# Denominators before the units, low halves of h on VectorE, and attention spread over the feed-forward units of a fused kernel

## The reference

```python
x = x + tanh(g_xattn[0]) * wkv(w, u, layernorm(x), ctx)          # linear recurrence over 64 steps
x = x + tanh(g_ffn[0]) * ffn(layernorm(x))                       # ternary weights, silu(gate) * up, rms_norm, projection
x = x + tanh(g_xattn[1]) * attention(layernorm(x), ctx, mask)    # 64 x 64 scores for each batch, softmax
x = x + tanh(g_ffn[1]) * linear(fp8(layernorm(x)))               # one scale over all of x
```

## Time and profile before

| what | value |
|---|---|
| three timed runs | 156.12, 156.14, 159.84 us; median 156.14 |
| the profiled execution | 155.57 us, of which the span is 153.8 us |
| PE busy | 121.0 us (79%) |
| DVE busy | 110.1 us (72%) |
| ACT busy | 93.9 us (61%) |
| POOL busy | 38.6 us (25%) |

### The profile page before, as it was taken

The page is one execution under the profiler, slowest core; times in us unless marked ns, Lnnn a source line. Parts: engine busy times, 40 slices in busy tenths (PEclk is TensorE's granted clock), DMA queues, the critical chain, the costliest instruction groups (busy, mean ns, idle before and its releaser), DMA issues. The chain is left out here.

```text
span 153.8 us, 2193 instructions
## 1 busy us (share of the span) xinstructions
PE 121.0 (79%) x733; PEld 79.1 (51%) x743; DVE 110.1 (72%) x263; ACT 93.9 (61%) x170; POOL 38.6 (25%) x80
## 2 busy tenths in 40 slices
PE   6998789729989999959689966977796897764751
PEld 6986663305335556524355645644555674532550
DVE  5879997979999999648664733405649659967940
ACT  3477695255778688895576536599548736318211
POOL 7807000077000000002505370200235612110600
PEclk9999999955999999995999999999999999999999
DMA  5999900000000000000000000000000000000224
GB/s 152 291 364 362 303 18 0 0 0 0 0 0 4 2 0 0 0 0 0 4 0 2 2 4 0 0 0 0 0 0 4 0 0 0 0 2 2 69 72 136
DMA packets 7094, 6.90 MB, mean 45 GB/s; under 512 B 1320, under 2 KB 6826, under 8 KB 7082
## 3 DMA queue, kind: packets, MB, share of 16 engines
q1 hardware_dynamic: 7072, 6.75, 13.7%
q10 hardware_dynamic: 10, 0.00, 0.0%
HBM read 5.70 MB, written 1.05 MB: 44 GB/s over the span
## 5 line engine op out<-in xcount | busy, mean ns | idle before, releaser
L1235 DVE SCALAR_TENSOR_TENSOR hbuf<-ps,pscale,sil 128x512 f32<-128x512 f32 x16 | 11.9, 746 | 20.6 <-ACT sil L573 15.5
L845 PE MATMUL ps<-wT,xhi 128*128 128x512 bf16 x60 | 23.7, 395 | 1.2 <-ACT xlo L545 0.7
L846 PE MATMUL ps<-wT,xlo 128*128 128x512 bf16 x60 | 23.5, 392 | 0.3 <-issue 0.2
L406 POOL TENSOR_SCALAR ve<-mv 128x2 f32<-128x2 f32 (+2 forms) x12 | 2.9, 239 | 68.8 <-DVE mv L1117 68.6
L904 PE MATMUL ps<-wT,wgu_raw 128*128 128x256 bf16 x128 | 16.6, 273 | 0.7 <-ACT wgu_raw L586 0.7
L573 ACT ACTIVATE sil<-ps 128x512 f32<-128x512 f32 x16 | 9.5, 596 | 10.7 <-PE ps L846 10.5
L586 ACT ACTIVATE wgu_raw<-ps 128x512 f16<-128x512 f32 x16 | 9.5, 596 | 6.9 <-PE ps L884 6.9
L1111 DVE BATCH_NORM_STATS2 stats<-xs 128x6 f32<-128x256 f32 x32 | 12.3, 415 | 1.9 <-DMA xs<-in_x_dram 1.5
L904 PEld LDWEIGHTS ps<-wT,wgu_raw 128*128 128x128 f16 x128 | 12.4, 98 | 2.2 <-ACT wgu_raw L586 1.0
L1123 DVE TENSOR_SCALAR xn<-xs,mv,rstd 128x256 f32<-128x256 f32 x26 | 10.5, 446 | 3.5 <-POOL rstd L407 2.5
L534 ACT ACTIVATE wscale<-ps 128x1024 bf16<-128x1024 f32 x6 | 6.1, 1023 | 7.9 <-PE ps L767 7.9
(11 more groups left out here) (167 smaller groups left out, 266.8 us busy)
## 6 DMA issues: line engine op xcount, KB each, us to landing
wgu_raw<-in_L_ffn_w_gate_up_dram SPq DMA_DIRECT2D x4, 512.0 KB, 9.5
ctx_sb<-in_ctx_dram SPq DMA_DIRECT2D x2, 512.0 KB, 8.7
wp_raw<-in_L_ffn_w_proj_dram SPq DMA_DIRECT2D x1, 1024.0 KB, 10.4
out_dram<-xs SPq DMA_DIRECT2D x4, 256.0 KB, 2.1
xs<-in_x_dram SPq DMA_DIRECT2D x2, 256.0 KB, 2.7
xs<-in_x_dram SPq DMA_DIRECT2D x1, 512.0 KB, 8.0
wlin_raw<-in_L_ffn_weight_dram SPq DMA_DIRECT2D x1, 256.0 KB, 9.1
bias_bc<-in_L_ffn_bias_dram SPq DMA_DIRECT2D x1, 128.0 KB, 8.7
```

The costliest lines, as they stand in the source:

```text
L845: pe.matmul(ps[:, bank, :], xhi[:, h, c, o:o + P], w, start=(c == 0), stop=False)
L846: mm = pe.matmul(ps[:, bank, :], xlo[:, h, c, o:o + P], w, start=False, stop=(c == CH - 1))
L1235: dve.scalar_tensor_tensor(out=hbuf[:, b, :], in0=ps[:, 1 + b, :], scalar=pscale[:, 0:1], in1=sil[:, b, :], op0=ALU.mult, op1=ALU.mult).th ...
```

## The change

- **Denominators first.** The denominator scan and bonus of pieces 2 and 3 (`den_scan`, `den_bonus`) run on DVE before the units, and ACT runs `invert(2)` and `invert(3)` before the first silu. `rest_in(2)` moves behind `silu(0)`. Both table loads of iteration 5 go. The numerators (`num_scan`, `num_bonus`) and `wkv_out` run in iterations 3 and 4, `quant` of matrix 5 in iteration 5, `y_back(1)` in iteration 5 instead of 6, `mix_pair(2)` in 5.
- **Low halves on DVE.** For units 8 to 15 `h_left` on PE and `h_low` on ACT are gone; DVE subtracts the high half from the bank itself.
- **Tanh gates.** For units 11 to 15 ACT computes tanh(gate / 2), and `gate_product` on DVE makes (tanh + 1) * gate of it; `pscale_half` carries the factor 1/2. One table set (`exp_and_others`), loaded once in iteration 11, serves these gates and all softmax exponentials. The two loads of iteration 12 and the one after the units go.
- **Attention spread.** The two attention groups that ran in iterations 10 to 14 by pairs are spread singly over iterations 9 to 15; `ffn_in(2)` and `ffn_in(3)` stand before `h_back`, the second one in iteration 9 instead of 8. `softmax_out(1)`, `attn_out(1)` and `part_stats(3, 1)` move behind the units.
- **POOL and DVE.** The masks and the clearing of `E` move from POOL to DVE in iteration 8; POOL's `bias_g` and `mean_square(2)` stand before its four weight parts, which now wait for the squares of unit 11.

```diff
-    EXP_UNIT = 12
+    LOW_DVE = 8
+    TANH_FROM = 11
...
+        th_ready = sem("th_ready")
+        halved = sem("halved")
         h_ready = sem("h_ready")
         hhi_ready = sem("hhi_ready")
         sq_ready = sem("sq_ready")
...
+            mean_square(2)
+            pool.wait_ge(in_bias, 16)
+            pool.tensor_scalar(bias_g[:, :], bias_bc[:, :], tg[:, 3:4], 0.0, ALU.mult, ALU.add).then_inc(bias_ready, 1)
...
+            power_and_shift(3, 0, 2, 1)
             power(2, 4, 2, 3)
             mean_square(3)
+            power(2, 6, 1, 4)
             mean_square(4)
-            power_and_shift(3, 0, 2, 1)
-            power(2, 6, 1, 4)
+            power(2, 7, 1, 5)
             power_and_shift(3, 2, 2, 2)
-            power(2, 7, 1, 5)
...
             rest_in(1)
+            invert(2)
             ln_apply(1, 0, TPC // 2, 1)
             xn_high(0)
             xn_high(1)
             xn_low(0)
             xn_low(1)
-            rest_in(2)
+            invert(3)
             act.preload_act_table_set("silu_and_others")
...
-                act.activation(sil[:, n % 2, :], ps[:, 0, :], ACT.Silu).then_inc(sil_ready, 1)
+                if n < TANH_FROM:
+                    act.activation(sil[:, n % 2, :], ps[:, 0, :], ACT.Silu).then_inc(sil_ready, 1)
+                else:
+                    act.activation(sil[:, n % 2, :], ps[:, 0, :], ACT.Tanh, scale=0.5).then_inc(th_ready, 1)
...
             for n in range(UNITS):
-                if n in (6, EXP_UNIT + 1):
-                    h_high(n - 1)
+                if n == TANH_FROM:
+                    act.preload_act_table_set("exp_and_others")
                 silu(n)
                 if n >= 1:
                     square(n - 1)
-                    if n not in (6, EXP_UNIT + 1):
-                        h_high(n - 1)
-                    h_low(n - 1)
+                    if n == 7:
+                        xn_high(2)
+                    if n == 9:
+                        xn_high(3)
+                    h_high(n - 1)
+                    if n - 1 < LOW_DVE:
+                        h_low(n - 1)
                 if n == 0:
+                    rest_in(2)
                     rest_in(3)
                 if n == 1:
                     rest_in(4)
@@ -627,42 +638,31 @@
                     rest_in(5)
                 if n == 4:
                     linear_weight()
-                if n == 5:
-                    act.preload_act_table_set("natural_log_exp_and_others")
-                    invert(2)
-                    invert(3)
-                    act.preload_act_table_set("silu_and_others")
                 if n == 7:
-                    xn_high(2)
                     xn_low(2)
-                if n == 8:
-                    xn_high(3)
+                if n == 9:
                     xn_low(3)
-                if n == 10:
                     channels_in(qT, 0, qT_ps, qT_ready)
                 if n == 11:
+                    softmax_exp(0)
                     channels_in(qT, 1, qT_ps, qT_ready)
-                if n == EXP_UNIT:
-                    act.preload_act_table_set("natural_log_exp_and_others")
-                    softmax_exp(0)
+                if n == 12:
+                    attn_in(0)
+                if n == 13:
                     softmax_exp(1)
-                    act.preload_act_table_set("silu_and_others")
-                if n == EXP_UNIT + 2:
-                    attn_in(0)
+                if n == 14:
                     attn_in(1)
             square(UNITS - 1)
             h_high(UNITS - 1)
-            h_low(UNITS - 1)
-            act.preload_act_table_set("natural_log_exp_and_others")
             channels_in(qT, 2, qT_ps, qT_ready)
             ln_apply(3, 0, 2, 2)
...
@@ -1015,13 +1015,32 @@
                 if n < UNITS:
                     gate(n)
                     up(n)
+                if n == 7:
+                    ffn_in(2)
+                if n == 9:
+                    ffn_in(3)
+                if n == 10:
+                    scores(0)
+                if n == 11:
+                    channel_major(2, 1, qT_ps)
+                if n == 12:
+                    probs_back(0)
+                    scores(1)
+                if n == 13:
+                    attend(0)
+                if n == 14:
+                    probs_back(1)
+                if n == 15:
+                    attend(1)
+                if n == UNITS + 1:
+                    channel_major(2, 2, qT_ps)
                 if 1 <= n <= UNITS:
                     h_back(n - 1)
                 if n >= 2:
                     project(n - 2)
-                if n == 6:
+                if n == 5:
                     y_back(1)
-                if 1 <= n <= UNITS:
+                if 1 <= n <= LOW_DVE:
                     h_left(n - 1)
...
                 if n == 7:
-                    ffn_in(2)
                     ffn_in_left(2)
-                if n == 8:
-                    ffn_in(3)
+                if n == 9:
                     ffn_in_left(3)
-                if n == 9:
                     channel_major(2, 0, qT_ps)
-                if n == 10:
-                    channel_major(2, 1, qT_ps)
-                    scores(0)
-                if n == 11:
-                    scores(1)
-                if n == EXP_UNIT + 1:
-                    probs_back(0)
-                    probs_back(1)
-                if n == EXP_UNIT + 2:
-                    attend(0)
-                    attend(1)
-
-            channel_major(2, 2, qT_ps)
+
             scores(2)
             channel_major(2, 3, qT_ps)
             residual_back(0)
+            probs_back(2)
             scores(3)
-            probs_back(2)
+            channel_major(2, 4, qT_ps)
+            attend(2)
             residual_back(1)
...
+            def den_scan(k):
+
+                dve.wait_ge(G_ready, k + 1)
+                dve.tensor_tensor_scan(sums[:, k, 0, :, :].rearrange("p b t -> p (b t)"), dec[:, k % CH, :],
+                                       kv[:, k, 0, :, :].rearrange("p b t -> p (b t)"), 0.0, ALU.mult,
+                                       ALU.add).then_inc(den_scanned, 1)
...
+            def num_scan(k):
+
+                dve.wait_ge(GV_ready, k + 1)
+                dve.tensor_tensor_scan(sums[:, k, 1, :, :].rearrange("p b t -> p (b t)"), dec[:, k % CH, :],
+                                       kv[:, k, 1, :, :].rearrange("p b t -> p (b t)"), 0.0, ALU.mult,
+                                       ALU.add).then_inc(scan_ready, 1)
...
+            def gate_product(n):
+
+                b = n % 2
+                dve.wait_ge(th_ready, n - TANH_FROM + 1)
+                dve.scalar_tensor_tensor(out=sil[:, b, :], in0=sil[:, b, :], scalar=1.0, in1=ps[:, 0, :],
+                                         op0=ALU.add, op1=ALU.mult).then_inc(sil_ready, 1)
+
+            def h_low(n):
+                dve.wait_ge(hhi_ready, n + 1)
+                dve.tensor_tensor(hlo[:, n % 2, :], ps[:, 3, :], hhi[:, n % 2, :], ALU.subtract).then_inc(hlo_ready, 1)
...
                 b = n % 2
+                if n >= TANH_FROM:
+                    gate_product(n)
+                if n == TANH_FROM:
+                    dve.wait_ge(halved, 1)
...
-                dve.scalar_tensor_tensor(out=hbuf[:, b, :], in0=ps[:, 1 + b, :], scalar=pscale[:, 0:1],
+                dve.scalar_tensor_tensor(out=hbuf[:, b, :], in0=ps[:, 1 + b, :], scalar=(pscale if n < TANH_FROM else pscale_half)[:, 0:1],
...
+            def masks():
+                dve.wait_ge(in_mask, 32)
+                dve.tensor_scalar(mask_f[:, :, :], mask_u8[:, :, :], 1.0, 0.0, ALU.mult, ALU.add).then_inc(mask_f_ready, 1)
+                dve.memset(E[:, :, :], 0.0).then_inc(E_0, 1)
+                dve.wait_ge(mask_f_ready, 1)
+                dve.tensor_scalar(mask_add[:, :, :], mask_f[:, :, :], -1.0, MASKED, ALU.add, ALU.mult).then_inc(mask_ready, 1)
...
+            den_scan(2)
             weights_scale()
-            wkv_product(2)
             mix_out()
             ln_stats(1, 0, TPC)
+            den_bonus(2)
             greatest_scales()
             ln_apply(1, TPC // 2, TPC // 2, 1)
+            den_scan(3)
+            den_bonus(3)
...
-            wkv_scan(2)
...
-                    wkv_bonus(2)
                 if n == 3:
+                    wkv_product(2)
                     wkv_product(3)
-                    wkv_scan(3)
+                    num_scan(2)
+                    num_bonus(2)
+                    wkv_out(2)
                 if n == 4:
-                    wkv_bonus(3)
+                    num_scan(3)
+                    num_bonus(3)
+                    wkv_out(3)
+                if n == 5:
                     quant_here(5)
                     quant_sign(5)
-                if n == 5:
-                    wkv_out(2)
-                    wkv_out(3)
-                if n == 6:
                     mix_pair(2)
                     ln_stats(1, 4, 2)
+                if n == 6:
```

(27 more changed lines are left out.)

34 lines of the change are left out of this document (22 added, 12 removed).

## The result

The changed kernel takes **144.31 us**, the median of four runs (143.94 to 146.07), against 156.95 for the kernel before beside it (156.12 to 159.84, four runs). The ratio is 0.923, with a 95% interval of 0.912 to 0.935. The forecast was 144.4. The kernel before took 154.2 to 162.6 us in the runs beside the experiments, longer at a lower mean granted clock (0.967: 154.8; 0.935: about 159.5; one at 0.73: 175.2, and one of b1_den_only at 0.74: 170.9), so a time is set only beside times taken with it.

A forecast was written before the change was run, and what follows sets the result against it. No engine bounds the whole; PE waits where its order meets ACT's, and DVE has room. Terms -0.8 - 2.2 - 5.4 - 3.8 + 0.5 = -11.7 from 155.57, plus 0.5 for the median: 144.4 us, range 142.0 to 148.5.

The forecast's parts named there:

- Stretch A, the front, +1.9: Up to gate(7): rest_in(2) behind the first silu makes PE wait, so gate(1) starts at 44.3 instead of 42.37, +1.9.
- The first rival: PE's clock falls in a new gap, before weight_rest(3), the first h_left or gate(8): 146.0, two falls 147.6; chance 0.20.
- The stall of iterations 5 and 6, -2.7: Before gate(7): both loads gone and y_back moved, PE runs without the old stall, gate(7) at 66.1 instead of 68.80.
- Stretch B, the clock of unit 7, -1.6: Gate(7) to gate(8): full clock for unit 7's gate and up, -1.6; the whole stretch 5.2 us instead of 7.4, -2.2.
- Stretches C and D: Gate(8) to gate(12), PE without waits, -5.4; gate(12) to the last project's end, DVE full, -3.8.
- The prices: Assumed DVE times: h_low 0.70, gate_product 0.75, each up to 1.0 for the range; masks 1.1 to 2.6 in iteration 8.
- The port, +0.5: Units 12 and 13: POOL's moved weight parts block some DVE operations with SBUF inputs, +0.5, between 0 and 4.
- The loads: Each removed ACT table load is worth 1.28 us; with the skill page's drain the sum would be 11.1 instead of 11.7.
- The tail, kept at 25.2: From the last softmax_in, at 116.4 instead of 128.63, to the end: order unchanged, the same length of 25.2 us.
- The total, 144.4: Whole kernel: -11.7 from the profiled 155.57 gives 143.9, plus 0.5 for the median of the runs; 7.5% less.

The follow-up runs named there:

- b1_den_only: The kernel before with only the early denominators and inversions and y_back(1) one iteration earlier: 154.2 us, ratio 0.969.
- a3_silu: The changed kernel with silu gates in all units, table loads around each softmax_exp and one after the units: 146.9 us.
- c1_relief: a4_warm with the low halves of units 13 and 14 on PE and ACT again: 144.2 us.
- a1_den_late: The changed kernel with denominators, inversions and their table loads, rest_in(2) and y_back(1) back at their old places: 150.6 us.
- b0_after_again: The changed kernel as it is, run again: 143.4 us, ratio 0.923.
- b1_den_again: The same kernel as b1_den_only, run once more for a profile: 154.4 us, ratio 0.990.
- b2_before_warm: The kernel before with matmuls that nobody reads added in three waits of PE: 158.7 us, ratio 1.004.
- d2_pairs: The changed kernel without the spreading: attention in the old places and pairs, low halves on DVE and tanh gates kept: 153.7 us.
- a4_warm: The changed kernel with 16 matmuls that nobody reads added in PE's two waits ahead of the units: 142.3 us, ratio 0.917.

## Why the prediction was right, point by point

- **Stretch A, the front, +1.9: the step right, its size right by luck.** Gate(1) came 2.35 later. The step "rest_in(2) now follows the silu ... PE has the next weight_rest queued behind up(0) ... and waits for it" is there in a3_silu (a wait of 0.91) and in c1_relief (1.50), and with a fall of the clock as short as before's it costs 1.6. In the profiled execution that met the forecast the rest, 0.8, is the low clock lasting to 42.7 instead of 38.3, and PE's own slow products hid most of the wait (0.18 left). At the full clock the order costs 0.15, because DVE holds up(0) in both orders; the prediction said that DVE does not hold PE here. A fall that lasts longer was no term of the sum. The first rival looked for a fall in a new gap; this one is longer in the old gap, and a1_den_late shows it with the old front. PE's wait ahead of the transposes does not set its length: 2.33 before and in a1_den_late, 2.50 in a3_silu, 2.23 in b0_after_again and b1_den_again, 3.03 after, and the low clock ends early, near 38.4, only in the kernel before and in a3_silu. What does set it is open.
- **The stall of iterations 5 and 6, -2.7: right**, and tested both ways (b1, a1). From gate(1) to gate(7) the changed kernel is 3.1 shorter, so that 0.4 more here made up for the 0.45 too much in the front.
- **Stretch B, the clock of unit 7, -1.6: the sum right, the cause incomplete.** The full clock alone earns 0.3 (b2_before_warm), since DVE's xn held gate(8). That xn was late because DVE waited 1.64 for a silu behind ACT's second load. The first part takes both loads away and puts one residual pair an iteration earlier, and in b1_den_again the transposes start without a wait; the prediction had a wait of 0.1 here and counted no gain. In the end the wait was 0.42, and the one for ACT's low half 0.96, as forecast: together -1.7 instead of -2.2.
- **Stretches C and D: right**, -5.38 and -3.7 for -5.4 and -3.8. DVE ran without a gap from 95.1 to 104.7 with 9.6 us of work (forecast 94.3, 104.2, 9.9), h_back(15) waited 1.04 ("about 1 us").
- **The prices.** h_low 0.68 (0.70), gate_product 0.67 (0.75), the masks 1.8, as 0.42, 0.91, 0.36 and 0.14 (1.1 to 2.6), off the path.
- **The port, +0.5: small, half of it seen.** In the stretch where the weight parts moved to, the products from PSUM kept their 0.69 and 0.75. One small operation was held, 0.47 where it takes 0.22 alone:

```profile
94.61 0.47 DVE L1321 SCALAR_TENSOR_TENSOR scoef<-sinv,tg,valid 128x2 f32<-128x2 f32 x1
...
95.11 0.69 DVE L1266 SCALAR_TENSOR_TENSOR sil<-sil,ps 128x512 f32<-128x512 f32 x1
95.84 0.75 DVE L1284 SCALAR_TENSOR_TENSOR hbuf<-ps,pscale_half,sil 128x512 f32<-128x512 f32 x1
...
93.81 1.25 POOL L431 TENSOR_TENSOR wp_raw<-wl,wl_parts 128x512 f32<-128x512 f32 x1
95.15 0.62 POOL L433 TENSOR_SCALAR wl_parts<-wp_raw 128x512 bf16<-128x512 f32 x1
95.85 1.16 POOL L435 TENSOR_TENSOR wl_parts<-wp_raw,wl_parts 128x512 bf16<-128x512 f32 x1
```

  This is what the Trainium skill, page "SBUF — State Buffer", section "Who interferes with whom", says of DVE instructions with at most one SBUF input, and the trace agrees (0.69 beside POOL, 0.67 on average).
- **The loads.** The trace and a3_silu show 1.28 us for each and the next function right behind. The drain of 1.38 us that the Trainium skill adds to every switch (page "ScalarE: Activation LUTs", section "What ACT_TABLE_LOAD costs") is not seen in any run here; the measurement decides.
- **The tail, kept at 25.2: right** (25.3). d2_pairs shows what it hung on: without the spreading DVE would have carried about 2.6 us more behind the last project.
- **The total, 144.4 for 144.31: closer than its terms.** The four stretches gave -11.5 and not -12.2, mostly by stretch B, and the port's +0.5 stands in the sum where only 0.25 was seen; the profiled execution went from 155.57 to 144.26, -11.3 for -11.7. The 0.57 by which the median lay above the profiled execution before was added, and after it is 0.05. Two errors of 0.4 and 0.5 offset each other there, and that is luck.

The parts do not add up singly. Taken out one at a time, by the middle columns and the tails, they are worth 5.2 (denominators), 1.7 less 0.8 behind them (low halves), 2.5 (tanh) and 1.1 + 4.4 + 4.1 (spreading, with the move of ffn_in; 1.5 of it a clock fall); alone, the first brings 4.7, and low halves and tanh on top of it 3.2 in the units and 2.7 back in the tail.

## What to carry to other kernels

The price of an order hangs on the clock of its stretch: the same front order cost 0.15 us at the full clock and 1.6 with a short fall. So compare two orders at a like clock, and look at the granted clock of a stretch before its starts are used as anchors. A slow stretch is worth what remains once the next engine's own lateness is counted; here 1.6 us of clock were worth 0.3. And when work is spread over iterations, look at what the other engines still carry when the loop ends: about 2.6 of 7 us of the gain were there.

## What the runs showed of the hardware

- The same wait of PE is followed by a low clock in one execution of the same kernel and not in another. The changed kernel, and then b0_after_again:

```profile
29.26 0.60 PE L765 MATMUL ps<-scales,group_spread 24*128 24x512 bf16 x1 [1.12 <-ACT wscale L535]
```

```profile
29.18 0.39 PE L765 MATMUL ps<-scales,group_spread 24*128 24x512 bf16 x1 [1.11 <-ACT wscale L535]
```

  Likewise behind waits of 2.18 and 2.24 the next products ran at 1.2 GHz in b2_before_warm and at 2.4 GHz in the kernel before.
- A fall costs about 1.7 us where the path is on PE (unit 13 and the last 24 products of b2_before_warm), and nothing where DVE comes later anyway: the 24 products at 130.98 of the changed kernel took 4.45 us at the low clock, and from its last softmax_in to the end it takes 25.3, as before.
- Products that nobody reads, put in the two waits of the front (16 of 0.22 us), kept the stretch from 28 to 43 us free of low slices in four of five profiled executions of kernels with such products there; in c1_relief the clock fell while PE ran them, and they took 4.45 instead of 2.76 us. The 142.3 us of a4_warm are the best found, 1 to 2 us under the changed kernel. The two were not timed on one chip, so the size is known only by their ratios to before, 0.917 (0.905 to 0.929) and 0.923, whose intervals overlap.
